# A mixed transformer block on one core: a WKV mix without its running maximum, and a quantised feed-forward stage whose rounding changes engine

## The reference, cut to what matters

```python
def step(carry, kv_t):
    p, q, o = carry
    kt, vt = kv_t
    no = jnp.maximum(o, u + kt)
    A = jnp.exp(o - no)
    E = jnp.exp(u + kt - no)
    y = (A * p + E * vt) / (A * q + E)
    no2 = jnp.maximum(w + o, kt)
    A2 = jnp.exp(w + o - no2)
    E2 = jnp.exp(kt - no2)
    return ((A2 * p + E2 * vt, A2 * q + E2, no2), y)
...
def activation_quant(x):
    scale = 127.0 / jnp.clip(jnp.max(jnp.abs(x), axis=-1, keepdims=True), EPS, None)
    return jnp.clip(jnp.round(x * scale), -128.0, 127.0) / scale
def weight_quant(w):
    scale = 1.0 / jnp.clip(jnp.mean(jnp.abs(w)), EPS, None)
    return jnp.clip(jnp.round(w * scale), -1.0, 1.0) / scale
...
x = x + wkv(w, u, layernorm(x), ctx_2048)
h = gelu(bitlinear(layernorm(x), w1), approximate=False)   # 256 -> 1024
x = x + bitlinear(h, w2)                                   # 1024 -> 256
```

## Time and profile before

| | |
|---|---|
| median of 3 runs | 579.8 us (576.61 to 581.23) |
| span of the profiled execution (first to last instruction) | 575.4 us |
| TensorE / VectorE / ScalarE / GpSimd busy | 381.8 / 337.8 / 161.9 / 238.7 us |
| mean granted TensorE clock | 0.801 |

### The profile page before, as it was taken

One profiled execution on the slowest core, in us unless ns is written; L12 is line 12 of the kernel. 1 busy time (PEld: TensorE's weight loads), 2 busy tenths in 40 slices (PEclk: granted clock), 3 DMA queues, 4 the chain that ended last, 5 costly groups with the idle time before them and its releaser, 6 DMA issues.

```text
span 575.4 us, 6820 instructions
## 1 busy us (share of the span) xinstructions
PE 381.8 (66%) x1909; PEld 268.8 (47%) x1910; DVE 337.8 (59%) x877; ACT 161.9 (28%) x333; POOL 238.7 (41%) x393
## 2 busy tenths in 40 slices
PE   0879985639869689995399959889980110013765
PEld 0658863426436356563278747668860000001433
DVE  3587667706436536525633517466423689999994
ACT  2323420122313213441033313223320251501343
POOL 2544534013414313551254596287006576370321
PEclk9989997758779859998589969889995555555787
DMA  8900392740530800000035603330002200000001
GB/s 289 408 8 0 102 155 73 136 48 2 73 37 20 108 5 18 2 19 19 23 92 198 173 9 137 128 128 18 27 27 76 61 18 1 1 0 0 10 28 36
DMA packets 24106, 39.07 MB, mean 68 GB/s; under 512 B 3312, under 2 KB 21040, under 8 KB 23056
## 3 DMA queue, kind: packets, MB, share of 16 engines
q1 hardware_dynamic: 18896, 30.63, 20.8%
q0 software_dynamic: 1872, 5.11, 3.3%
q10 hardware_dynamic: 3312, 3.02, 1.5%
HBM read 29.38 MB, written 9.31 MB: 67 GB/s over the span
## 4 chain that ended last, share of the span: by engine, by line
PE 41%; DVE 25%; DMA 15%; POOL 6%; issue 6%; SPq 4%; ACT 2%; POOLq 0%; DVEq 0%; ACTq 0%
DMA xg<-xn_dram,slot_tok 7%; PE bank L1392 6%; PE bank L1546 6%; PE bank L1393 5%; PE bank L1394 5%; DMA k_pack<-qk_dram 4%; PE bank L1398 3%; PE bank L1470 3%; SPq L427 2%; DVE den L1272 2%; POOL yc L605 2%; PE bank L1547 2%; PE bank L1532 2%; PE bank L1454 2%; DVE q_s L1306 2%
## 5 line engine op out<-in xcount | busy, mean ns | idle before, releaser
L566 POOL TENSOR_SCALAR_AFFINE_SELECT E_sb<-E_sb 128x128 f32<-128x128 f32 x64 | 22.4, 349 | 112.7 <-ACT E_sb L749 112.7
L1002 DVE CUSTOM_DVE_ANT_0 junk<-bank,causal 128x128 bf16<-128x128 f32 (+1 forms) x128 | 38.7, 354 | 51.5 <-PE bank L1470 51.4
L1179 DVE TENSOR_TENSOR act_lo<-bank,act_hi 128x512 fp32r<-128x512 f32 x23 | 15.9, 690 | 69.0 <-ACT act_hi L790 69.0
L749 ACT ACTIVATE E_sb<-bank 128x384 f32<-128x384 f32 x64 | 31.2, 490 | 72.2 <-PE bank L1533 72.0
L1392 PE MATMUL bank<-we_hi,xg_hi 128*128 x92 | 41.5, 451 | 8.8 <-POOL we_lo L557 8.1
L1546 PE MATMUL bank<-E_sb,v_aug 128*32 128x256 f32 x128 | 45.2, 449 | 0.0
L1393 PE MATMUL bank<-we_lo,xg_hi 128*128 x92 | 38.2, 416 | 0.0
L1394 PE MATMUL bank<-we_hi,xg_lo 128*128 x92 | 38.1, 414 | 0.0
L590 POOL DMA_INDIRECT xg<-xn_dram,slot_tok x23 | 22.0, 957 | 37.8 <-DMA xg<-xn_dram,slot_tok 22.2
L1532 PE MATMUL bank<-q_pack,k_pack 49*128 49x256 f32 x64 | 24.5, 396 | 15.8 <-DMA q_pack<-negmax_t 13.9
L557 POOL TENSOR_TENSOR we_lo<-we_lo,we_hi 128x3072 fp32r<-128x3072 f32 x5 | 33.8, 6756 | 0.4
(11 more groups left out here) (251 smaller groups left out, 1088.0 us busy)
## 6 DMA issues: line engine op xcount, KB each, us to landing
we_lo<-in_wexp SPq DMA_DIRECT2D x8, 1536.0 KB, 7.7
qk_dram<-qk_parts SPq DMA_DIRECT2D x8, 512.0 KB, 3.4
q_pack<-qk_dram SPq DMA_DIRECT2D x24, 128.0 KB, 4.7
k_pack<-qk_dram SPq DMA_DIRECT2D x24, 128.0 KB, 7.6
y_dram<-y_sb ACTq DMA_DIRECT2D x23, 128.0 KB, 1.7
we_hi<-in_w_t SPq DMA_DIRECT2D x2, 1024.0 KB, 10.1
ctx_sb<-in_ctx_t SPq DMA_DIRECT2D x1, 1024.0 KB, 7.2
xn_dram<-x_n SPq DMA_DIRECT2D x8, 128.0 KB, 1.7
```

The lines of the kernel that those rows point to most:

```text
L749: a.activation(E_sb[:, n % 4, :], bank[4 + n % 2][:, 0:3 * P], ACT.Exp).then_inc(exp_done, 1)
L1002: last = v.tensor_tensor_reduce(out=junk[:, m % 2, t * P:t * P + keys], in0=bank[(2 if b >= 1 else 0) + h % 2][:, t * P:t * P + keys], in1 ...
```

## The change

Stage C goes by batch. The running maximum is gone: the states p and q are plain decayed sums with a decay of exp(min(w, 0)), started from q = 1e-30 and p = 1e-30 v. TensorE puts the keys straight into a PSUM bank of the batch (a product with `ident`), onto a ramp -w t (one product of 512 columns from `w_row` and `t_row`). ScalarE makes two kinds of Exp from that bank. TensorE also makes the sums: q + e and p + e v, by two accumulating products with `ident` each, which turn them at the same time. VectorE inverts and multiplies in the layout of the tokens. In stage D, GpSimd rounds both q_h and q_g, the turns are in f32 (the constant stays in), and ScalarE's copy to bf16 subtracts it. The clipping at 127 is left out, since the scale bounds the values. q_g has three buffers, and TensorE works on q_g two steps behind q_h (`G_LAG`). The inverse is taken of unit = max(top, EPS)/127, once for both tiles.

The new streams, cut to what matters:

```diff
+            def load_splits(s):
+                return lambda: pe.reg_mov(splits, pe.value_load(slot_e[0:1, s], min_val=1, max_val=NE))
...
-                        pe.reg_load(*load)
+                        load()
...  (SP) one more small load, w_row, ahead of bonus_sb; in_small counts to 96
...  (GpSimd)
+            link(g.iota(t_row[:, :, :], pattern=[[0, KC], [1, S]], base=0, channel_multiplier=0,
+            g.affine_select(out=t_row[:, :, :], in_=t_row[:, :, :], compare_op=ALU.not_equal, fill=0.0,
...
+            def c_times_v(b):
+                pool.wait_ge(c_e, b + 1)
+                link(g.tensor_scalar(e, e, E_MAX, 0.0, ALU.min, ALU.max))
+                g.tensor_tensor(e_v[:, b % 2, :, :], e, values_of(b), ALU.mult).then_inc(c_ev, 1)
+            def d_round(step):
+                    g.tensor_scalar(q_h[:, step % 2, :], q_h[:, step % 2, :], q_inv[:, step, 0:1], MAGIC,
+                    g.tensor_scalar(q_g[:, i % 3, :], q_g[:, i % 3, :], q_inv[:, step, 1:2], MAGIC,
...             (after rsqrt(3, 4) and gather(7): c_times_v(0); after rsqrt(3, 5): c_times_v(1))
...  (ScalarE)
+            def c_exp(b):
+                act.wait_ge(c_tr, TB * (b + 1))
+                for k in range(KC):
+                    last = a.activation(e_now[:, b % 2, k, :], keys_of(b)[:, k, :], ACT.Exp, bias=e_bias[:, k:k + 1])
+                a.activation(bank[EXP_BANK[b]][:, :], bank[KEY_BANK[b]][:, :], ACT.Exp).then_inc(c_f, 1)
...
+            for step in range(NT + G_LAG):
+                if step < NT:
+                    d_h_copy(step)
+                    d_gelu_of(step)
+                if step >= G_LAG:
+                    d_g_copy(step - G_LAG)
...  (VectorE)
+            v.tensor_scalar(w_neg[:, :], decay_sb[:, :], 0.0, None, ALU.min)
+            v.scalar_tensor_tensor(e_bias[:, :], decay_sb[:, :], 0.0, bonus_sb[:, :], ALU.max, ALU.add)
+            v.tensor_scalar(w_row[:, :], w_row[:, :], -1.0, 0.0, ALU.mult, ALU.min).then_inc(wkv_row, 1)
...
+            def c_scans(b):
+                dve.wait_ge(c_f, b + 1)
+                for k in range(KC):
+                    last = v.tensor_tensor_scan(q_st[:, b, k, 1:S + 1], w_exp[:, k:k + 1].to_broadcast([P, S]),
+                                                f[:, k, :], Q_FIRST, ALU.mult, ALU.add)
+                link(v.tensor_tensor(fv, f, values_of(b), ALU.mult))
+                for k in range(KC):
+                    last = v.tensor_tensor_scan(p_st[:, b, k, 1:S + 1], w_exp[:, k:k + 1].to_broadcast([P, S]),
+                                                fv[:, k, :], 0.0, ALU.mult, ALU.add)
+            def c_result(i):
+                link(v.reciprocal(r, bank[i % 2][:, D:2 * D]))
+                link(v.tensor_tensor(r, bank[i % 2][:, 0:D], r, ALU.mult))
+                link(v.tensor_tensor(x_sb[:, i, :], x_sb[:, i, :], r, ALU.add))
...
+            def d_scales(step):
+                    link(normalise(h, 4, step, x_sb[:, step, :]))
+                    last = v.tensor_reduce(q_top[:, step, 0:1], h, AX, ALU.max, apply_absolute_value=True)
+                    last = v.tensor_reduce(q_top[:, step, 1:2], q_g[:, i % 3, :], AX, ALU.max, apply_absolute_value=True)
+                link(v.tensor_scalar(q_unit[:, step, part], q_top[:, step, part], EPS, 1.0 / 127.0, ALU.max, ALU.mult))
+                v.reciprocal(q_inv[:, step, part], q_unit[:, step, part]).then_inc(d_inv, 1)
+                v.tensor_tensor(q_deq[:, step, part], q_unit[:, step, part], wmean[:, part], ALU.mult).then_inc(d_deq, 1)
...
+            c_combine(0)
+            for i in range(1, 5):
+                c_combine(i)
+                c_norm(i - 1)
+            c_scans(0)
+            for i in range(5, 7):
+                c_combine(i)
+                c_norm(i - 1)
+            c_scans(1)
+            c_combine(7)
+            for i in range(6, 8):
+                c_norm(i)
+            for i in range(2):
+                c_result(i)
+            c_scans(2)
+            for i in range(2, 4):
+                c_result(i)
+            c_scans(3)
+            for step in range(NT + G_LAG):
+                d_scales(step)
+                if step + 4 < NT:
+                    c_result(step + 4)
+                if step >= 5:
+                    d_last(step - 5)
...  (TensorE)
+            for i in range(5):
+                c_keys(i)
+            for i in range(2):
+                c_result(i)
+            for i in range(5, NT):
+                c_keys(i)
+            for i in range(2, 6):
+                c_result(i)
+            for step in range(NT + G_LAG + 1):
+                if step < NT:
+                    d_h_turn(step)
+                    d_up_products(step)
+                if step >= G_LAG + 1:
+                    d_down_products(step - G_LAG - 1)
+                if G_LAG <= step < NT + G_LAG:
+                    d_g_turn(step - G_LAG)
+                if step < 2:
+                    c_result(step + 6)
```

More of the change, by code:

```diff
@@ L1349, in d_last @@
                     dve.wait_ge(out_done[i % 2], 16 * (i // 2))
-                v.scalar_tensor_tensor(x_out[:, i % 2, :], bank[6 + i % 2][:, 0:D], q_s[:, 1, i, 2:3],
-                                       x_sb[:, i, :], ALU.mult, ALU.add).then_inc(d_out, 1)
-            c_tiles(0)
-            for st, init in ((o_st, -1e38), (p_st, 0.0), (q_st, 0.0)):
-                last = v.memset(st[:, :, :, 0:1], init)
-            link(last)
-            for k in range(KC):
-                c_exponents(0, k)
@@ L1700, in _ @@
                 m_iteration(s, s % 2, more=NSLOT - 1 - s)
[L1703 to L1720 removed]
+            pe.wait_ge(m_yc, NSLOT)
@@ new lines, in _, with c_keys @@
+            pe.wait_ge(wkv_row, 1)
+            def c_keys(i):
+                b, tt = i // TB, i % TB
+                dst = keys_of(b)
+                if tt == 0:
+                    t_.matmul(dst, w_row[:, :], t_row[:, :, :], start=True, stop=False)
+                pe.wait_ge(c_h, i + 1)
+                for k in range(KC):
+                    last = t_.matmul(dst[:, k, tt * P:(tt + 1) * P], hc[:, i % 2, k * P:(k + 1) * P], ident[:, :],
+                                     start=False, stop=(tt == TB - 1 and k == KC - 1))
+                last.then_inc(c_tr, 1)
@@ new lines, in c_result @@
+            def c_result(i):
+                b, tt = i // TB, i % TB
+                if tt == 0:
+                    pe.wait_ge(c_pq, b + 1)
+                    pe.wait_ge(c_ev, b + 1)
+                if i >= 2:
+                    pe.wait_ge(stats_in[4], i - 1)
+                cols = slice(tt * P, (tt + 1) * P)
+                for j, (st, now) in enumerate(((q_st, e_now), (p_st, e_v))):
+                    for k in range(KC):
+                        dst = bank[i % 2][:, (1 - j) * D + k * P:(1 - j) * D + (k + 1) * P]
+                        t_.matmul(dst, st[:, b, k, cols], ident[:, :], start=True, stop=False)
+                        last = t_.matmul(dst, now[:, b % 2, k, cols], ident[:, :], start=False, stop=True)
```

402 lines of the change are left out of this document (134 added, 268 removed).

## The result

The changed kernel took 542.84 us (median of 4, 535.29 to 547.33); the kernel before, beside it, 580.51 (median of 4, 576.61 to 586.35). The ratio is 0.9285, interval 0.919 to 0.9379. Two more sets of runs of the same changed kernel gave 0.9333 (0.9278 to 0.9388) and 0.9345 (0.9211 to 0.9478). The change gains some 7%; 555 had been forecast, with 545 as the low end. The direction was right, the time was not: the three sets have medians of 542.8, 538.6 and 545.1, all some 10 us or more under 555. That the first lies 2.2 us under the low end of the range is within what one set differs from the next; the third would have been just inside it.

What follows compares the result with a forecast made beforehand. VectorE was taken as the bound from the first WKV scan to the last tiles. Span 575.4 − 28.3 (stages) + 0.8 (start) + 3.0 (expert loop) = 550.9, plus 4.4 gives 555.3 us; range from 545 to a little past 572.

Steps and rivals of the forecast that it cites:

- The ring: Quantised stage: h_copy, up, down, g_turn, g_copy on TensorE and ScalarE set the step; 4.5 to 7.1 us, 5.3 taken.
- Scans: WKV stage, VectorE: two scan pairs a batch at 1.27 us each; with product and links 13.4 us for four batches.
- the slow-scan rival: WKV stage: VectorE stays slow beside GpSimd, scans cost 21.4 us, + 8, time 563; chance 0.10.
- VectorE's list: WKV stage from hc at 453.3 through result(7): 57.7 us, including waits and 3 for GpSimd beside VectorE, ending at 511.0.
- Path of the fifth step: Quantised stage: scales(4), round, turn, copy, then up, down and turn take 7.3 us, to 518.3.
- Expert loop: TensorE's stream: the asserted load's added instructions cost 0.15 us in each of 21 slots, +3 us; bounds 0 and 7.4.
- Start: First loads: one more small load delays the last one that VectorE waits for, +0.8 us; bounds 0 and +1.5.
- Around the span: Whole kernel: the median lies 4.4 us above the profiled span, added to 550.9 to give 555.3.
- Half clock: WKV and quantised stages: TensorE stays at 1.2 GHz, time 570; chance 0.16.
- slow loop: Expert loop: the asserted load stops TensorE's stream in each slot, 1.75 us a slot, 37 in all, 589; chance 0.05.
- The signs: New profile: first gather at 434 + 4, last combine before 468, inverses 1.7 us, scan pairs 1.3, VectorE idle some 2 a step.
- Everything hides, 545: TensorE at 2.4 GHz from the first result, no contention, expert loop unchanged: 4.0, 3.0 and 3.0 us less; chance 0.13.

Runs made afterwards that it cites:

- Experiment 8: Changed kernel with exp(k) written by ScalarE to SBUF instead of a PSUM bank: 540.7 us, one run.
- experiments 5: Changed kernel with TensorE's turn of g ahead of the down products: 534.0 us, again 543.0; with h one step ahead from the fifth step also: 535.9.
- experiment 6: Changed kernel with two unread ScalarE passes of 512 behind each copy of g from the fourth step on: 552.0 us, ratio 0.9522.
- 7: Changed kernel with an unread VectorE product of 512 behind each d_scales: all ten steps 550.8 us, again 547.1; last six steps 549.8.
- Experiment 2: Kernel before with the asserted load of splits alone: 573.9 us, ratio 0.9953; changed kernel with that load made twice: 540.5 us, ratio 0.9358.
- experiment 4: Changed kernel with the next tile's turn and copy of h ahead of g's turn and copy, all steps: 544.5 us, ratio 0.9478.

## Why the prediction was wrong, point by point

The span was forecast as 93.8 of tail (547.1 − 453.3), 3.8 of additions ahead of it, and 4.4 around it. Found: 86.4, about 0, and 1.7. Take 7.4, 3.8 and 2.7 from 555.3 and 541.4 is left; 542.84 was measured, and the other 1.4 is less than two sets of one kernel differ by. The ring is the largest single term of the miss, 4.6 us, but not the whole of it: with the ring alone put right the forecast would have been 550.7.

- **Scans.** Right: pairs of 1.25 against 1.27, in every batch. The reserve of 3 us for GpSimd beside VectorE was too large. What was stretched was one sum in `c_result` (1.19 instead of 0.43), two normalises (0.81 instead of 0.40) and a combine (1.33 instead of 1.00), 1.9 us. Experiment 8 shows that the slow-scan rival was a real mechanism, kept away by the PSUM source. The 8 us that it was priced at supposed all four batches; the edit hit one pair.
- **VectorE's list** to the last result: 57.7 forecast, 55.5 found (514.74 − 459.2). A result takes 3.25 us instead of 3.05; the waits were 1.41 and 0.72 for inverse roots, 2.1 against 2.5, and not for TensorE, as I had thought for norm(7).
- **Path of the fifth step:** 7.3 forecast; from 514.74 to the end of the turn of g at 521.75, 7.0. The agreement is in part luck. The chain of waits doesn't go this way: h's turn is done at 518.35, but ScalarE gets to its copy at 518.5 only, behind the copy of g, whose turn stood at 1.2 GHz. The path that counted and VectorE's ended 0.2 to 0.3 us apart.
- **The ring.** The step of the prediction that failed by most is "so I expect a mixture, nearer the upper: 5.3". The mechanism was right: the ring was named with its members and order, and experiments 5, 6 and 7 confirm it from three sides. Its size was 4.24, at the upper level in all three rounds (4.5 forecast for that level; that the tails of the products overlap more may be the rest). The lower level stood one step earlier, where it cost nothing that the tail shows. Three rounds, 12.7 against 15.9, and the drain 3.10 against 3.8 a step: 4.6 of the 7.4 us. The argument for the mixture was a window of before in which 54% of a step at the upper level was followed by a step at 0.66. The changed kernel's window 523 to 531 has 5.78 of 8.00 busy at 1.00, and no fall follows. In experiment 6 a window with 3.44 of 6.00 busy and a gap of 2.27 us was followed by a fall. The forecast had itself worked out 66% for the ring at the upper level and then went by a window of before with 54%; what decides the level stays open here, since the same gap of 2.79 us was followed by a fall in some records and not in others.
- **Expert loop:** +3.0 forecast, "I take 0.15 each". Experiment 2 finds it within 0.03 a slot. The late weight load said less of TensorE's lead than I took from it.
- **Start:** +0.8 forecast. The chain at the start of the changed kernel:

```profile
4.83 5.69 DMA bonus_sb<-in_bonus
...
11.76 0.34 DVE a_lo L937
```

  It passes a_lo at 11.76, not later than the 13.15 of the earlier trace rows, but the kernel with the asserted load alone passes it at 11.44, as its load landed early too. The landing moves between 10.3 and 12.9 us over the seventeen executions; the change adds the three short operations, 0.27, and an issue of 0.4. What it costs can't be told from that scatter.
- **Around the span:** "The median shown lies 4.4 above the profiled span" set the median over several executions against the span of one. In every run that has both, 1.7 to 2.2 us lie around the span. The profiled execution of before was one of the shorter ones, by 2 to 3 us; that is scatter, not an offset.
- **Half clock, slow loop:** TensorE's mean clock was 0.66 to 0.67 through the WKV stage, where VectorE bounds anyway, and it was at the upper level in the three rounds that count. The slower case fell with experiment 2.
- **The signs:** "gathers later than 440 (then the loop or the start has grown)" and "the last combine before 468" pointed the wrong way. In the profiled execution the first gather was issued at 440.20 and the last combine came at 471.33; in the two others of the same kernel it was 433.29 and 432.40, and about 464 both times. A time counted from the start holds the scatter of the head. The signs read inside the tail (inverses of 1.7, pairs of 1.3, VectorE idle 2 us a step while TensorE waits for ScalarE) all came true.
- **Everything hides, 545**, came nearest, at 0.13. Its price of the ring, 0.8 less a round, was short of the 1.06 found, and it kept the 4.4. With 1.7 in its place the case stands at 542.3, so this one term is all that put the measured time outside the range. The range ended exactly on it, with no reserve below for terms that were all rounded up: the additions, the contention and the mixture each had their chosen value above the lower bound.

## What to carry to other kernels

When a bound engine is relieved, look for the ring of two engines behind it, add up its members, and look at their order: one group of products moved out of the ring took some 4 us more off the tail here, for no work saved. Price each unknown at its own place, but then ask what the sum does if all of them come out at the low bound, for chosen values that all lean one way make a range that ends too early. And take a kernel's difference from the stage that changed, where it repeats within 1 us, and the offset around the span from one and the same execution.

## What the runs showed of the hardware beyond that

- In a ring of two engines, TensorE's level can make a small addition dear. 1.05 us more of ScalarE's work in a round cost 1.0 in the first and 2.7 in each of the next two, where the level fell just after a gap of 2.27 us. In the changed kernel gaps of 1.23 to 1.46 us in every round of 4.24 left it at 2.4 GHz.
- A wait before a fall can come from an order: in experiment 4 the turn of h waited 1.93 us at the head of TensorE's queue, and the turn of g behind it took 1.91 us instead of 1.04. But a gap of 2.79 us in the fourth step was followed by a fall in the three records of the changed kernel, and by none in experiment 6 and in one of two records of the turn of g first, where every operation up to there is the same.
- A scan from PSUM beside GpSimd's product takes 1.25 us a pair; the same pair from SBUF takes 2.28 and slows GpSimd's product from 1.27 to 1.72. A sum of two SBUF tensors beside that product takes 1.19 or 1.38 instead of 0.43, when the two happen to meet.
- Nothing in the head was changed but the register load and the few operations of the start, and still the end of it moved by 17 us between executions, more than most of the effects studied. TensorE was busy 344 us in the head that ended at 444.2 and 361 us in the one that ended at 459.2, but 343 in before's 453.3. The granted clock goes with it at the ends: 0.88 and 0.87 over the two shortest heads, 0.83 over the two longest, 0.84 to 0.87 over the rest in no clear order. Most of the difference lies early: the first copy of an expert result (L799) starts at 295.9 us in the execution with the shortest head and at 311.2 in the one with 459.2. Whether the clock is the cause isn't shown.
